# Routing one-hots in 16-bit pairs, filling products in two groups, and a small gather issued early in a two-layer mixture-of-experts kernel

## What is computed

```python
x = x + 0.5 * ffn(layernorm(x))     # mixture of experts, top 2 of 8, hidden size 512
x = x + attn(layernorm(x))          # causal, 16 heads of 16
x = x + 0.5 * ffn(layernorm(x))     # the same weights again

def ffn(x):                          # x: 1024 x 256
    logits = x @ router_weight.T
    top_vals, top_idx = top_k(logits, 2)
    gates = softmax(top_vals)        # 0 for the other experts
    for each expert: h = x @ w_in.T; a, b = split(h); o = silu(a) * b @ w_out.T
        acc += gate[:, None] * o
    return acc + bias
```

## Time and profile before

| | us |
|---|---|
| Median of 3 runs | 429.79 (428.55 to 430.70) |
| The profiled execution | 432.28 |
| Its span, first to last instruction | 430.5 |
| TensorE busy | 403.6 (94%) |
| VectorE busy | 302.0 (70%) |
| ScalarE busy | 257.6 (60%) |
| GpSimd busy | 248.1 (58%) |
| Mean granted TensorE clock | 0.975 of full |

### The profile page before, as it was taken

One profiled execution on the slowest core, in us unless ns is written; L12 is line 12 of the kernel. 1 busy time (PEld: TensorE's weight loads), 2 busy tenths in 40 slices (PEclk: granted clock), 3 DMA queues, 4 the chain that ended last, 5 costly groups with the idle time before them and its releaser, 6 DMA issues.

```text
span 430.5 us, 10146 instructions
## 1 busy us (share of the span) xinstructions
PE 403.6 (94%) x2899; PEld 331.7 (77%) x2900; DVE 302.0 (70%) x610; ACT 257.6 (60%) x640; POOL 248.1 (58%) x308
## 2 busy tenths in 40 slices
PE   7879999899999989799999999898799999999996
PEld 3548888788888857588888888774588888888885
DVE  5797997756566797777678576968355675556666
ACT  2737865466555454788787787732255555565552
POOL 5146457775568259547767678200454586745860
PEclk9689999999999999989999999988999999999999
DMA  7929931112121620000000000006651212111226
GB/s 267 389 71 384 385 107 39 56 43 73 49 49 37 224 82 0 1 2 2 4 1 0 0 0 0 0 2 225 199 187 50 52 37 74 54 56 49 49 73 244
DMA packets 22026, 38.90 MB, mean 90 GB/s; under 512 B 3184, under 2 KB 14704, under 8 KB 21744
## 3 DMA queue, kind: packets, MB, share of 16 engines
q1 hardware_dynamic: 17168, 24.41, 16.4%
q0 software_dynamic: 4544, 12.07, 9.3%
q10 hardware_dynamic: 288, 2.10, 1.3%
HBM read 29.37 MB, written 9.19 MB: 90 GB/s over the span
## 4 chain that ended last, share of the span: by engine, by line
PE 65%; DVE 19%; DMA 5%; issue 5%; ACT 2%; POOL 2%; DVEq 0%; ACTq 0%; POOLq 0%; SPq 0%
PE bank L1351 25%; PE bank L1373 13%; PE bank L1521 6%; PE bank L1532 4%; PE bank L1361 4%; PE bank L1488 3%; PE bank L1327 2%; DMA w_out<-y_scratch 2%; DVE x L1048 2%; DVE arena L883 2%; DMA arena<-xn_scratch,gather_row 2%; DMA y_scratch<-arena,scatter_row 1%; DVE pT_lo L1159 1%; PE bank L1522 1%; DVE v L1229 1%
## 5 line engine op out<-in xcount | busy, mean ns | idle before, releaser
L516 POOL DMA_INDIRECT arena<-xn_scratch,gather_row x46 | 51.6, 1121 | 65.5 <-PE bank L1327 38.9
L522 POOL DMA_INDIRECT y_scratch<-arena,scatter_row x42 | 60.6, 1443 | 33.9 <-ACT arena L688 30.8
L1017 DVE TENSOR_TENSOR wo_lo<-w_out,wo_hi 128x1024 fp32r<-128x1024 f32 x46 | 61.5, 1337 | 3.9 <-PE bank L1373 2.4
L1351 PE MATMUL bank<-w_hi,xT_hi 128*128 x184 | 62.0, 418 | 0.0
L1022 DVE TENSOR_TENSOR gT_lo<-bank,gT_hi 128x512 fp32r<-128x512 f32 x46 | 31.7, 690 | 38.8 <-ACT gT_hi L662 38.8
L1351 PE MATMUL bank<-w_hi,xT_lo 128*128 x184 | 57.6, 394 | 0.0
L1351 PE MATMUL bank<-w_lo,xT_hi 128*128 x184 | 57.3, 392 | 0.0
L600 POOL TENSOR_TENSOR k_head<-k_hi,head_mask 128x256 fp32r<-128x256 f32 x64 | 38.7, 625 | 29.1 <-PE bank L1522 22.2
L655 ACT ACTIVATE arena<-bank 128x512 f32<-128x512 f32 x46 | 27.5, 597 | 46.4 <-PE bank L1351 44.4
L677 ACT ACTIVATE wo_hi<-w_out 128x1024 fp32r x46 | 48.8, 1060 | 5.6 <-issue 3.8
L1006 DVE TENSOR_TENSOR xT_lo<-bank,xT_hi 128x256 fp32r<-128x256 f32 x46 | 19.5, 424 | 35.4 <-ACT xT_hi L647 29.4
(11 more groups left out here) (192 smaller groups left out, 964.8 us busy)
## 6 DMA issues: line engine op xcount, KB each, us to landing
w_raw<-in_win_t SPq DMA_DIRECT2D x8, 1024.0 KB, 10.1
w_out<-in_wout_t SPq DMA_DIRECT2D x16, 512.0 KB, 7.8
w_out<-y_scratch SPq DMA_DIRECT2D x8, 512.0 KB, 5.7
xn_scratch<-arena ACTq DMA_DIRECT2D x2, 1024.0 KB, 6.3
x<-in_x SPq DMA_DIRECT2D x4, 256.0 KB, 3.5
out<-x SPq DMA_DIRECT2D x4, 256.0 KB, 2.1
arena<-xn_scratch,gather_row POOLq DMA_INDIRECT x46
y_scratch<-arena,scatter_row POOLq DMA_INDIRECT x46
```

The costliest lines, as they stand in the source:

```text
L516: pool.indirect_dma_start(out=xb[j % 2][:, :], out_offset=None, in_=xn_dram, in_offset=bass.IndirectOffsetOnAxis(ap=gather_row[:, j:j + 1] ...
L522: pool.indirect_dma_start(out=y_dram, in_=y[j % 2][:, :], in_offset=None, out_offset=bass.IndirectOffsetOnAxis(ap=scatter_row[:, j:j + 1], ...
L1017: dve.tensor_tensor(wo_lo[:, :, :], w_out[:, bass.ds(e, 1), :, :].rearrange("p o c d -> p (o c) d"), wo_hi[u][:, :, :].bitcast(F32), ALU.s ...
L1351: last = pe.matmul(bank[2 * half + u][:, :], tok[u][:, k, :], wts[:, bass.ds(e, 1), k, half * H:(half + 1) * H], start=(part == 0 and k == ...
```

## The change

Three things change.

1. The one-hots. All operands of lines 952, 969 and 971 become fp16. The numbers compared with are the new constants row_nos (128) and blk_nos (24, one more than there are blocks, so that the count is even). Each value is stored twice side by side: row_twice by an added copy (`tensor_copy` from row_i), block_twice by the addition of line 967, and pair_id as a constant of 16 x 2. Each operation is now written over the shape pairs x (numbers / 2) x 2, in which the innermost two elements lie side by side in every operand. blk_hot and blk_pair are 24 wide; the products of line 1317 read 23 of them.
2. The filling products. WARM_RANKS becomes ((6, 5), (6, 5)): six, a wait for the new semaphore half_hot, which the first half of the row one-hots signals, then five, then the wait for hot_ready.
3. `rehearse`. Behind its last constant GpSimd writes 128 numbers (own_row) and issues an indirect gather of 128 rows of 8 words of the router's weights into unused_rows, which nothing reads. Ahead of its waits for the first layer's plan it waits for that gather (rehearsed).

Declarations of the new tiles and semaphores are left out here.

```diff
@@ -51,7 +51,7 @@
 LOOPED = (BLOCKS - 2 - PEELED) // 2
 AFTER = PEELED + 2 * LOOPED
 EARLY = 3
-CONSTS = 22
+CONSTS = 24
 IDENT_CONSTS = 3
 KSLOTS = 2
 P_SCALE = 2.0 ** 15
...
@@ -67,7 +67,7 @@
 POOL_LEAD = 1
 BIAS_STEP = 4
 
-WARM_START, WARM_RANKS, WARM_PLAN, WARM_TURNED = 12, (11, 18), (6, 6), (4, 4)
+WARM_START, WARM_RANKS, WARM_PLAN, WARM_TURNED = 12, ((6, 5), (6, 5)), (6, 6), (4, 4)
 WARM_END, WARM_TURN2, WARM_CHOSEN = 2, 2, 2
 WARM_TURN = (5, 3)
 WARM_LN = (5, 1, 0, 0)
...
@@ -166,8 +166,8 @@
         xn_late = view(arena, at, [TILES, D])[0]
         xnT, at = view(arena, at, [DK, T])
         row_hot, at_hot = view(arena, at, [PAIRS, P], F16)
-        blk_hot, at_hot = view(arena, at_hot, [PAIRS, BLOCKS])
-        blk_pair, at_hot = view(arena, at_hot, [PAIRS, BLOCKS], F16)
+        blk_hot, at_hot = view(arena, at_hot, [PAIRS, BLOCKS + 1], F16)
+        blk_pair, at_hot = view(arena, at_hot, [PAIRS, BLOCKS + 1], F16)
 
         xb, y = [None] * 2, [None] * 2
         at = 0
...
@@ -468,6 +476,12 @@
                 then(pool.affine_select(out=t, in_=t, pattern=pattern, compare_op=op, fill=fill, base=base,
                                         channel_multiplier=mult))
 
+            def rehearse():
+
+                then(pool.iota(own_row[:, :], [[0, 1]], base=0, channel_multiplier=1))
+                pool.indirect_dma_start(out=unused_rows[:, :], out_offset=None, in_=wr_in,
+                                        in_offset=bass.IndirectOffsetOnAxis(ap=own_row[:, 0:1], axis=0)).then_inc(rehearsed, 16)
+
             def inverse_root(phase, first=0, pairs=1):
                 pool.wait_ge(var_ready, TPAIRS * phase + first + pairs)
                 some = slice(2 * first, 2 * (first + pairs))
...
@@ -493,7 +507,9 @@
             iota(tile_edge[:, :], [[1, TILES]], 0, 0)
             then(pool.tensor_scalar(tile_edge[:, :], tile_edge[:, :], 1.0 / TILES, None, ALU.mult))
             inverse_root(0, 3)
-            iota(pair_id[:, :].rearrange("p (k i) -> p k i", k=TOPK), [[T, TOPK], [1, TILES]], 1, TILES)
+            iota(pair_id[:, :, :].rearrange("p (k i) b -> p k i b", k=TOPK), [[T, TOPK], [1, TILES], [0, 2]], 1, TILES)
+            iota(row_nos[:, :], [[1, P]], 0, 0)
+            iota(blk_nos[:, :], [[1, BLOCKS + 1]], 0, 0)
             iota(trash_id[:, :], [[P, BLOCKS]], TOPK * T + 1, 1)
             then(pool.memset(neg_mask[:, :], 0.0))
             select(neg_mask[:, :], [[-1, P]], 0, 1, ALU.is_ge, NEG)
...
@@ -502,6 +518,7 @@
             select(head_mask[:, :], [[-HD, HPC]], 0, 1, ALU.is_ge, 0.0)
             select(head_mask[:, :], [[HD, HPC]], HD - 1, -1, ALU.is_ge, 0.0)
             assert steps[0] == CONSTS
+            rehearse()
 
             def add_bias(phase, b, first=0, pairs=TPAIRS):
 
...
@@ -550,6 +567,8 @@
                 ins.then_inc(slot_hot_ready, 1)
 
             def ffn(f):
+                if f == 0:
+                    pool.wait_ge(rehearsed, 16)
                 pool.wait_ge(plan_ready, f + 1)
                 pool.wait_ge(xn_stored, 16 * (f + 1))
                 if f:
...
@@ -947,14 +966,19 @@
                 dve.wait_ge(route_step, over_at)
                 first_at = mark(dve.tensor_reduce(first_block[:, :], over_edge[:, :, :], AX_X, ALU.add))
 
-                def one_hot_rows(q):
-                    shape = [P, q.stop - q.start, P]
-                    return mark(dve.tensor_tensor(row_hot[:, q, :], bc(row_i[:, q], 2, shape), bc(col[:, :], 1, shape),
-                                                  ALU.is_equal))
+                def in_twos(a):
+                    return a.rearrange("p (n b) -> p n b", b=2)
+
+                def one_hot(to, q, values, numbers):
+                    shape = [P, q.stop - q.start, to.shape[2] // 2, 2]
+                    return dve.tensor_tensor(to[:, q, :].rearrange("p q (n b) -> p q n b", b=2),
+                                             bc(values[:, q, :], 2, shape), bc(in_twos(numbers[:, :]), 1, shape), ALU.is_equal)
 
 
                 dve.wait_ge(route_step, row_at)
-                one_hot_rows(slice(0, PAIRS // 2))
+                row_at = mark(dve.tensor_copy(row_twice[:, :, :], bc(row_i[:, :], 2, [P, PAIRS, 2])))
+                dve.wait_ge(route_step, row_at)
+                one_hot(row_hot, slice(0, PAIRS // 2), row_twice, row_nos).then_inc(half_hot, 1)
                 dve.wait_ge(route_step, first_at)
                 placed_at = mark(dve.tensor_tensor(placed[:, :, :, :], choice[:, :, :, :],
                                                    first_block[:, :].unsqueeze(1).unsqueeze(1).to_broadcast(both), ALU.mult))
...
@@ -962,14 +986,16 @@
                 dve.wait_ge(route_step, placed_at)
                 block_at = mark(dve.tensor_reduce(block_of[:, :].rearrange("p (k i) -> p k i", k=TOPK), placed[:, :, :, :],
                                                   AX_X, ALU.add))
-                one_hot_rows(slice(PAIRS // 2, PAIRS))
+                one_hot(row_hot, slice(PAIRS // 2, PAIRS), row_twice, row_nos)
                 dve.wait_ge(route_step, block_at)
-                block_at = mark(dve.tensor_tensor(block_of[:, :], block_of[:, :], blk_i[:, :], ALU.add))
+                twice = [P, PAIRS, 2]
+                block_at = mark(dve.tensor_tensor(block_twice[:, :, :], bc(block_of[:, :], 2, twice), bc(blk_i[:, :], 2, twice),
+                                                  ALU.add))
                 dve.wait_ge(route_step, block_at)
-                then(dve.tensor_tensor(blk_hot[:, :, :], bc(block_of[:, :], 2, [P, PAIRS, BLOCKS]),
-                                       bc(block_no[:, :], 1, [P, PAIRS, BLOCKS]), ALU.is_equal))
-                dve.tensor_tensor(blk_pair[:, :, :], blk_hot[:, :, :], bc(pair_id[:, :], 2, [P, PAIRS, BLOCKS]), ALU.mult)\
-                    .then_inc(hot_ready, 1)
+                then(one_hot(blk_hot, slice(0, PAIRS), block_twice, blk_nos))
+                dve.tensor_tensor(blk_pair[:, :, :].rearrange("p q (n b) -> p q n b", b=2),
+                                  blk_hot[:, :, :].rearrange("p q (n b) -> p q n b", b=2),
+                                  bc(pair_id[:, :, :], 2, [P, PAIRS, (BLOCKS + 1) // 2, 2]), ALU.mult).then_inc(hot_ready, 1)
 
                 dve.wait_ge(route_step, end_at)
                 past_at = mark(dve.tensor_tensor(past[:, :, :], bc(end_block[:, :], 1, [P, BLOCKS, E]),
...
@@ -1311,10 +1337,12 @@
                 for i in range(TILES):
                     last = pe.matmul(bank[6][:, 0:E], ones[:, :], chosen[:, i, :], start=(i == 0), stop=(i == TILES - 1))
                 last.then_inc(ranks_done, 1)
-                warm(WARM_RANKS[f])
+                warm(WARM_RANKS[f][0])
+                pe.wait_ge(half_hot, f + 1)
+                warm(WARM_RANKS[f][1])
                 pe.wait_ge(hot_ready, f + 1)
                 for q in range(PAIRS):
-                    last = pe.matmul(bank[7][:, 0:BLOCKS], row_hot[:, q, :], blk_pair[:, q, :], start=(q == 0),
+                    last = pe.matmul(bank[7][:, 0:BLOCKS], row_hot[:, q, :], blk_pair[:, q, 0:BLOCKS], start=(q == 0),
                                      stop=(q == PAIRS - 1))
                 last.then_inc(pairs_done, 1)
 
```

More of the change, by code:

```diff
@@ L196, in build @@
         block_no = sb("block_no", [P, BLOCKS])
-        pair_id = sb("pair_id", [P, PAIRS])
+        row_nos = sb("row_nos", [P, P], F16)
+        own_row = sb("own_row", [P, 1], I32)
+        unused_rows = sb("unused_rows", [P, E])
+        blk_nos = sb("blk_nos", [P, BLOCKS + 1], F16)
+        pair_id = sb("pair_id", [P, PAIRS, 2], F16)
         trash_id = sb("trash_id", [P, BLOCKS])
@@ L229, in build @@
         row_i = sb("row_i", [P, PAIRS], I32)
+        row_twice = sb("row_twice", [P, PAIRS, 2], F16)
+        block_twice = sb("block_twice", [P, PAIRS, 2], F16)
         blk_i = sb("blk_i", [P, PAIRS], I32)
@@ L276, in build @@
         hot_ready = sem("hot_ready")
+        half_hot = sem("half_hot")
+        rehearsed = sem("rehearsed")
         pairs_done = sem("pairs_done")
```

## The result

| | kernel before | changed kernel |
|---|---|---|
| Median of 21 runs, us | 432.32 | 429.57 |
| Lowest to highest, us | 427.77 to 434.46 | 427.38 to 431.01 |
| Profiled execution, its span, us | 432.28, 430.5 | 430.32, 428.6 |

What follows compares the result with a forecast made beforehand. Matmuls on TensorE set the pace almost everywhere, but each feed-forward layer's routing waits for VectorE. Savings of 1.75 us (first layer) and 1.10 (second) sum to 2.85, taking 429.79 to 426.9 us; range 425.7 to 429.9.

Steps and rivals of the forecast that it cites:

- the halved slope: VectorE's comparisons and product take two elements a cycle: row one-hot 0.53 us less, block steps 0.18 less, 1.20 per routing.
- the other end: VectorE's comparisons stay at one element a cycle, without doubling: each routing 0.26 us longer.
- (a): No doubling: VectorE takes the pairs at one element a cycle; 429.8 us, 15%.
- (b): VectorE's doubled rate throttled by rereading one 32-bit value word; 0.48 us saved per routing, 428.3 us, 6%.
- (d): VectorE pays for each broken run of two 16-bit words; slower, 438.2 us, 6%.
- the 0.45 that was priced: Routing's filling products on TensorE: a late filler costs at most one of them, 0.45 us.
- the term of 0.55: First layer's first gather: rehearsal removes a first-use delay between plan and issue, 0.55 us; ends 0 and 1.08.
- Lands long before 22 us: The rehearsal's gather of 128 short rows lands well ahead of the plan, so its wait is over by then.
- What is next late: Section on what follows the routing: VectorE's weight splits still allow 1.75 us in the first layer; 1.10 in the second.
- the loads' tail: Second layer's first gather lands at the tail of the weight loads, costing 0.1 us, 0.5 at most.
- the term at 1.10: Second layer's whole gain, after the cost of the weight loads: 1.10 us.
- (c): TensorE's clock falls on the first layer's first block after a longer idle, costing 1.8 us; 428.7 us, 8%.

Runs made afterwards that it cites:

- no_twos: Changed kernel with each value stored once and reread at a step of 0, still 16-bit; row one-hot 1221 ns, one execution in 435.30 us.
- changed_again: The changed kernel itself, run again in a second series beside its variants; ratio 0.998 to the kernel before.
- few_loads: Changed kernel with one w_out load instead of four queued ahead of the second layer's first gathers; ratio 0.9924 to the kernel before, four slow runs left out.
- passed_early: Changed kernel with one w_out load ahead and expert 0's weights signalled before the other seven loads are issued; median 428.64 us, ratio 0.9938 to the kernel before.
- best_passed: As passed_early, plus the rehearsal's wait moved behind the first layer and 12 and 10 fillers behind the plan; 426.84 us, ratio 0.9903 to the kernel before.
- best_of_all: Changed kernel with one load ahead, rehearsal's wait behind the first layer, 12 and 10 fillers behind the plan; ratio 0.9989 to the kernel before.
- old_few_loads: Kernel before with only one w_out load ahead of the second layer's first gathers; ratio 1.0081 to the kernel before.

## Why the prediction was right or wrong

**The comparisons: right, to the hundredth.** 0.69 and 0.36 us as forecast, the plan 1.20 us earlier behind the ranks in both layers of the first profile (6.46 to 5.25). The row for the halved slope was the right one, and no_twos measured the other end as worked out. Rivals (a), (b) and (d) are out: no row of 0.69 us leaves room for a throttle on the value word that is read repeatedly. Line 1229, which served as a bound, has one operand in fp32 (v_rest), so it said less of a kernel with all operands in 16 bits than it was taken for. The rule of the Trainium skill (VectorE: DVE Perf Modes, The perf-mode tier table (the rule you actually need)), whose column is for bf16, holds for this form in fp16 too: the trace agrees, with 686 ns.

**The fillers: right in kind, not always free.** The half-way wait costs nothing and 18 fillers would have cost 1.11 us. But where the clock stayed down until 20.7 us (changed_again, first layer), eleven fillers ended late and the plan took 5.51 us: 0.25 us, within the 0.45 that was priced. This came in six of the 14 first layers with the new comparisons and fillers (5.39 to 5.53 us).

**The rehearsal: the term of 0.55 was 0.3, and its mechanism isn't shown.** The forecast took the 0.55 us between the two layers' delays (0.83 against 0.28) for a cost of first use that the rehearsal removes. It removed 0.11 of it and shortened what follows by 0.15 to 0.2. The rest goes with the form of the wait: 0.77 us with the plan's wait on an instruction of its own, 0.28 with it on the gather, wherever the rehearsal landed. "Lands long before 22 us" was wrong too: 7.52 us for 4 KB, at 21.37, 0.2 us behind the plan. The share of the DMA engines around its issue was about 1.0, which could have told me that a small transfer would not get through quickly; but the traces in which it landed early show that this cost nothing. In "What is next late" I looked at VectorE's splits and not at ScalarE's, which ended at 26.24 us and let xT_hi begin just then.

**The second layer: the step that failed most.** The forecast took 0.1 us off for the loads' tail, "0.5 at most", and so put the term at 1.10. I had looked at where the tail ended in one trace (303.2 us) and set the new issue beside it, but did not ask how the tail stands to the plan when TensorE's clock differs in the router products ahead. The tail took 0.1, 1.1 and 0.5 us in the three profiles, and 1.12, 0.09 and 0.73 us were left at the turn, 0.65 on the mean. That the first profile came out at 1.12 is luck of its clock. Only with the loads taken away did it come to 1.2 whichever clock the router products had (9.76 to 8.51, 8.54 and 8.59 in few_loads, passed_early and best_passed, and 8.72 in best_of_all).

**The clock.** Rival (c) was given 8% and 1.8 us; the fall showed in the first layer of two of three profiles, as (c) had it, at 1.5 us, and in the second layer of two as well. But it also falls on the old routing (old_few_loads), so it is a spread of the totals more than a cost of the change; whether the change made it more frequent is open.

**The sum.** From the ranks to the turn the three profiles of the changed kernel gain 1.51, 1.23 and 1.48 us in the first layer, where 1.75 was forecast, and 1.12, 0.09 and 0.73 in the second: 2.6, 1.3 and 2.2 us in all, against 2.85 forecast and 0.6 to 2.2 us by the three ratios. The sign was right and the size too large, by the second layer's term first and the rehearsal's next.

**The level.** 429.57 us lies in the range of 425.7 to 429.9, but that says little: the forecast of 426.9 was counted down from 429.79, the median of three runs, and 21 runs of the kernel before have 432.32. With that start the same saving gives 429.5. So the time came out 2.7 us above the forecast nearly all because of the start, and the hit on the range is luck as much as insight; the size of the saving is judged by the ratios and the stretches.

## What to carry to other kernels

When a serial step is made shorter, look for what arrives next, on the DMA queues as well as on the engines: here the transfers issued ahead of it held the gather's landing and kept up to 1.1 of 1.2 us, and fewer loads ahead gave it back. Then look at who waits for the signal of the loads you moved. Before a short delay is put down to first use, look at which instruction holds the wait in either case: the same gather went out 0.28 us behind the plan when it held the plan's wait itself, and 0.77 when another instruction ahead of it did.

## What the runs showed of the hardware

A comparison of two 16-bit tensors took 686 ns for 1024 elements when the innermost two elements lay side by side in every operand, though one operand was a single pair read 64 times over, and 1221 ns when that operand was a single element at a step of 0. An indirect gather's generation on GpSimd took 0.94 to 1.10 us with VectorE idle and 1.48 to 1.98 us beside its stream of subtractions from SBUF to SBUF. The gather went out 0.28 us behind the plan when it held the plan's wait itself, and 0.77 to 0.88 us behind it when a separate waiting instruction stood ahead; one of 4 KB issued 20 us earlier changed nothing in that. A gather of 4 KB took 6.4 to 8.0 us to land among queued weight loads. A gather issued while the tail of 3 MB of queued transfers was in the DMA engines led to the turn 3.5 to 4.2 us after its issue in six traces, and 3.0 to 3.2 with the loads taken away.
